# Cross-attention on one core: scores as fp32 matmuls on row halves, projections as 64-column tiles, both placed behind the scores of a step

## The reference, cut to what matters

```python
# x: (1, 1024, 128), ctx: (1, 6404, 128), 16 heads of 64, all fp32
Q, K, V = x @ W_Q, ctx @ W_K, ctx @ W_V        # split into 16 heads of 64 columns
scores = einsum('bhqd,bhkd->bhqk', Q, K) / 8
attn = softmax(scores)                          # over 6404 keys
context = einsum('bhqk,bhkd->bhqd', attn, V)
out = context @ W_O + x
return (out - mean) / sqrt(var + 1e-5)
```

## Time and profile before

| | |
|---|---|
| time, median of 3 runs | 1790.04 us (1789.16 to 1790.11) |
| span of the profiled execution | 1789.5 us |
| around the span | 0.5 us by the median; the page has no time of its own for the profiled execution |
| TensorE busy, share of the span | 99% |
| DVE, ACT busy | 71%, 52% |
| granted TensorE clock, mean | 0.998 (2.4 GHz level) |

### The profile page before, as it was taken

The page is one execution under the profiler, slowest core; times in us unless marked ns, Lnnn a source line. Parts: engine busy times, 40 slices in busy tenths (PEclk is TensorE's granted clock), DMA queues, the critical chain, the costliest instruction groups (busy, mean ns, idle before and its releaser), DMA issues.

```text
span 1789.5 us, 23718 instructions
## 1 busy us (share of the span) xinstructions
PE 1767.2 (99%) x7814; PEld 973.5 (54%) x7814; DVE 1266.8 (71%) x1376; ACT 931.8 (52%) x1079; POOL 21.3 (1%) x24
## 2 busy tenths in 40 slices
PE   9999999999999999999999999999999999999997
PEld 4555555555555555555555555555555555555555
DVE  5667667668667686667876677676786677776687
ACT  5555555555555555545555554555555555555552
POOL 0000000000000000000000000000000000000000
PEclk9999999999999999999999999999999999999999
DMA  2000000000000000000000000000000000000000
GB/s 80 12 18 18 13 21 18 12 18 12 22 18 18 12 22 15 17 18 12 22 18 12 18 18 17 18 18 12 18 22 12 18 18 12 16 18 12 18 1 13
DMA packets 25022, 31.41 MB, mean 18 GB/s; under 512 B 6384, under 2 KB 12528, under 8 KB 24944
## 3 DMA queue, kind: packets, MB, share of 16 engines
q1 hardware_dynamic: 24256, 29.78, 6.2%
q10 hardware_dynamic: 688, 0.66, 0.1%
HBM read 29.90 MB, written 0.52 MB: 17 GB/s over the span
## 4 chain that ended last, share of the span: by engine, by line
PE 98%; DVE 1%; issue 0%; DMA 0%; ACT 0%; POOLq 0%; POOL 0%; ACTq 0%
PE s_ps L442 44%; PE o_ps L453 41%; PE v_ps L430 5%; PE kq_ps L419 5%; PE kq_ps L425 1%; PE v_ps L577 0%; DMA xT_sb<-in_xT 0%; PE kq_ps L577 0%; DVE inv_sum L897 0%; PE o_ps L593 0%; DVE limits L841 0%; PE o_ps L425 0%; PE v_ps L593 0%; PE kq_ps L593 0%; PE s_ps L425 0%
## 5 line engine op out<-in xcount | busy, mean ns | idle before, releaser
L697 ACT ACTIVATE probs<-s_ps 128x1024 f32<-128x1024 f32 x816 | 793.0, 1024 | 777.8 <-PE s_ps L442 755.2
L828 DVE TENSOR_TENSOR sums<-sums,probs 128x1024 f32<-128x1024 f32 (+1 forms) x800 | 935.0, 1218 | 3.7 <-issue 0.5
L442 PE MATMUL s_ps<-q_parts,k_parts 128*128 128x512 f32 x3264 | 860.4, 405 | 7.5 <-DVE inv_sum L897 6.1
L453 PE MATMUL o_ps<-probs,v_ring 128*64 128x512 f32 x3264 | 746.3, 599 | 0.0
L442 PEld LDWEIGHTS s_ps<-q_parts,k_parts 128*128 128x128 f32 x3264 | 576.9, 188 | 285.8 <-issue 170.5
L453 PEld LDWEIGHTS o_ps<-probs,v_ring 128*64 128x64 f32 x3264 | 215.8, 136 | 419.0 <-issue 417.9
L815 DVE COPY v_ring<-v_ps 128x256 f32<-128x256 f32 (+1 forms) x209 | 87.4, 418 | 473.4 <-PE v_ps L430 473.4
L430 PEld LDWEIGHTS v_ps<-wv_sb,ctx_ring 128*128 128x128 f32 x816 | 123.4, 190 | 64.8 <-issue 56.1
L430 PE MATMUL v_ps<-wv_sb,ctx_ring 128*128 128x128 f32 x816 | 124.5, 274 | 0.0
L419 PE MATMUL kq_ps<-ctx_ring,wk_sb 128*128 128x512 f32 (+1 forms) x208 | 104.9, 586 | 0.0
L797 DVE TENSOR_TENSOR k_parts<-kq_ps,k_parts 64x512 fp32r<-64x512 f32 (+1 forms) x104 | 70.0, 673 | 9.7 <-ACT k_parts L682 6.5
(11 more groups left out here) (54 smaller groups left out, 112.5 us busy)
## 6 DMA issues: line engine op xcount, KB each, us to landing
ctx_ring<-in_ctxT SPq DMA_DIRECT2D x96, 256.0 KB, 2.6
ctx_ring<-in_ctxT SPq DMA_DIRECT2D x8, 130.0 KB, 2.4
wq_dup<-in_wq SPq DMA_DIRECT2D x14, 64.0 KB, 2.1
wk_sb<-in_wk SPq DMA_DIRECT2D x8, 64.0 KB, 2.3
wv_sb<-in_wv SPq DMA_DIRECT2D x8, 64.0 KB, 2.8
xT_sb<-in_xT ACTq DMA_DIRECT2D x1, 512.0 KB, 6.1
x_sb<-in_x SPq DMA_DIRECT2D x1, 512.0 KB, 5.4
wo_sb<-in_wo SPq DMA_DIRECT2D x1, 512.0 KB, 6.4
```

The source lines that it names most:

```text
L442: last = nc.tensor.matmul(s_ps[:, head, q], k_parts[:, head, cols:cols + P], q_parts[:, parity, head, part, q], start=(part == 0), stop=(p ...
L453: last = nc.tensor.matmul(o_ps[rows, q], v_ring[:, v_at[0], v_at[1], rows], p_view[:, p_slot, head, q], start=start, stop=stop)
L697: nc.scalar.activation(p_view[:, p_slot, head, :], s_ps[:, head, :], ACT.Exp, scale=SCALE).then_inc(probs_ready, 1)
L828: nc.vector.tensor_tensor(out=sums[0:rows, parity, head, :], in0=sums[0:rows, parity, head, :], in1=p_view[0:rows, p_slot, head, :], op=AL ...
```

## The change

Scores become plain fp32 matmuls on row halves: K of head 0 lies in rows 0 to 63 and K of head 1 in rows 64 to 127 of one tile `k_sb`, Q likewise in `q_sb`. `s_ps` is now ordered by half of the queries, then head, and `scores`, the exponentials and the sums go by half of the queries (both heads of it) where they went by head. The high and low parts and everything that made them are gone: one copy on ACT takes a projection (`take_k`, `take_q`). Each projection is two 64-column matmuls in place of one of 128 columns; Q of the next pair takes two such pairs in place of four whole matmuls, at steps c and c+4 of the straight part. In TensorE's order both score blocks come first, then the projection, then V:

On ACT the copy of a projection comes behind the exponentials of both chunks, on DVE the copy of V behind the sums of A. The diff, cut to its core:

```diff
-            uses.update({(c, "mid"): ("q", 0), (c, "end"): ("q", 1), (c + 4, "mid"): ("q", 2),
-                         (c + 8, "mid"): ("q", 3), (c + 10, "mid"): ("k", 0)})
+            uses.update({(c, "mid"): ("q", 0), (c + 4, "mid"): ("q", 1), (c + 10, "mid"): ("k", 0)})
...
-        k_parts = sb("k_parts", [P, 2, RING_COLS], F32R)
-        q_parts = sb("q_parts", [P, 2, 2, 2, NQ], F32R)
+        k_sb = sb("k_sb", [P, RING_COLS])
+        q_sb = sb("q_sb", [P, 2, NQ])
...
-        q0_ps = [o_ps[:, 0:QH], o_ps[:, QH:NQ], s_ps[:, 1, 0:QH], s_ps[:, 1, QH:NQ]]
+        q0_ps = [o_ps[:, 0:QH], o_ps[:, QH:NQ]]
...
-                for copy in range(2):
-                    sp.dma_start(wq_dup[:, parity, :, copy, :], src_q).then_inc(w_loaded[parity], 16)
+                sp.dma_start(wq_sb[:, parity, :], w_q[:, cols]).then_inc(w_loaded[parity], 16)
...
-                nc.tensor.matmul(kq_ps[:, 0:n], wk_sb[:, parity, :], ctx_ring[:, b_slot * BK:b_slot * BK + n],
-                                 start=True, stop=True).then_inc(kq_proj_done, 1)
+                for head in range(2):
+                    rows = slice(head * DH, (head + 1) * DH)
+                    last = nc.tensor.matmul(kq_ps[rows, 0:n], wk_sb[:, parity, rows],
+                                            ctx_ring[:, b_slot * BK:b_slot * BK + n], start=True, stop=True)
+                last.then_inc(kq_proj_done, 1)
...
             def project_v(pos, cols, parity):
-                return nc.tensor.matmul(v_ps[:, pos * P:(pos + 1) * P], ctx_ring[:, cols:cols + P],
-                                        wv_sb[:, parity, :], start=True, stop=True)
+                for half in range(2):
+                    keys = slice(half * DH, (half + 1) * DH)
+                    last = nc.tensor.matmul(v_ps[keys, pos * P:(pos + 1) * P],
+                                            ctx_ring[:, cols + half * DH:cols + (half + 1) * DH],
+                                            wv_sb[:, parity, :], start=True, stop=True)
+                return last
...
             def scores(cols, parity, exps_before):
-                for head in range(2):
+                for h in range(NQH):
                     if exps_before is not None:
-                        pe.wait_ge(probs_ready, exps_before + head + 1)
-                    for h in range(NQH):
-                        q = slice(h * QH, (h + 1) * QH)
-                        for part in range(2):
-                            last = nc.tensor.matmul(s_ps[:, head, q], k_parts[:, head, cols:cols + P],
-                                                    q_parts[:, parity, head, part, q],
-                                                    start=(part == 0), stop=(part == 1))
+                        pe.wait_ge(probs_ready, exps_before + h + 1)
+                    for head in range(2):
+                        rows = slice(head * DH, (head + 1) * DH)
+                        last = nc.tensor.matmul(s_ps[:, h, head * QH:(head + 1) * QH], k_sb[rows, cols:cols + P],
+                                                q_sb[rows, parity, h * QH:(h + 1) * QH], start=True, stop=True)
                     last.then_inc(scores_ready, 1)
...
                 def step(c, k, looped):
                     todo = chunks_of(c, k)
-                    chunk_scores(*todo[0], looped)
+                    for following in todo:
+                        chunk_scores(*following, looped)
                     projection(c, k, looped, "mid")
...
                     group.then_inc(v_proj_done, 1)
-                    if len(todo) > 1:
-                        chunk_scores(*todo[1], looped)
...
-                nc.scalar.activation(k_parts[0:DH, 0, cols], kq_ps[0:DH, 0:n], ACT.Copy)
-                nc.scalar.activation(k_parts[DH:P, 1, cols], kq_ps[DH:P, 0:n], ACT.Copy).then_inc(kq_high_ready, 1)
+                nc.scalar.activation(k_sb[:, slot * BK:slot * BK + n], kq_ps[:, 0:n], ACT.Copy).then_inc(kq_taken, 1)
...
-                        if n == 0:
-                            high_halves(c, k, looped, "mid")
-                    high_halves(c, k, looped, "end")
+                    take_projection(c, k, looped, "mid")
+                    take_projection(c, k, looped, "end")
...
-            def low_k(slot):
-            def low_q(src, n, parity):
```

More of the change, by code:

```diff
@@ new lines, in project_k @@
+                last.then_inc(kq_proj_done, 1)
+            def project_q(dst, n, parity):
+                for head in range(2):
+                    rows = slice(head * DH, (head + 1) * DH)
+                    last = nc.tensor.matmul(dst[rows, :], wq_sb[:, parity, rows], xT_sb[:, n * QH:(n + 1) * QH],
+                                            start=True, stop=True)
+                last.then_inc(kq_proj_done, 1)
+            def project_v(pos, cols, parity):
+                for half in range(2):
[4 more added lines that the diff above has]
+                return last
@@ L452, in pv @@
                         rows = slice(head * DH, (head + 1) * DH)
-                        last = nc.tensor.matmul(o_ps[rows, q], v_ring[:, v_at[0], v_at[1], rows], p_view[:, p_slot, head, q],
-                                                start=start, stop=stop)
+                        last = nc.tensor.matmul(o_ps[rows, q], v_ring[:, v_at[0], v_at[1], rows],
+                                                p_view[:, p_slot, h, head * QH:(head + 1) * QH], start=start, stop=stop)
                 last.then_inc(pv_done, 1)
@@ L467, in _ @@
             project_k(0, 0, None)
-            pe.wait_ge(wq0_loaded, 32)
+            pe.wait_ge(wq0_loaded, 16)
             pe.wait_ge(x_loaded, 16)
-            for n in range(4):
+            for n in range(NQH):
                 project_q(q0_ps[n], n, 0)
@@ L569, in pair_body @@
                     if h == 0:
-                        pe.wait_ge(kq_split, use(pair, LOOP_USES + len(straight_uses(last)) - 1))
+                        pe.wait_ge(kq_taken, use(pair, LOOP_USES + len(straight_uses(last)) - 1))
                     else:
@@ L584, in w_need @@
                 if first:
[L585 to L586 removed]
+                    return 48
+                return 24 * pair + (16 + 24 if parity else 48)
             run_pairs(pe, pair_body)
@@ L818, in add_sums @@
             def add_sums(g, p_slot, parity, new, rows):
-                for head in range(2):
-                    dve.wait_ge(probs_ready, 2 * g + head + 1)
+                for h in range(NQH):
+                    dve.wait_ge(probs_ready, NQH * g + h + 1)
                     if new:
-                        nc.vector.tensor_copy(sums[:, parity, head, :], p_view[:, p_slot, head, :]).then_inc(sums_done, 1)
+                        nc.vector.tensor_copy(sums[:, parity, h, :], p_view[:, p_slot, h, :]).then_inc(sums_done, 1)
                     else:
-                        dve.wait_ge(sums_done, 2 * g + head + (SUM_CREDIT - 1))
-                        nc.vector.tensor_tensor(out=sums[0:rows, parity, head, :], in0=sums[0:rows, parity, head, :],
-                                                in1=p_view[0:rows, p_slot, head, :], op=ALU.add).then_inc(sums_done, 1)
+                        dve.wait_ge(sums_done, NQH * g + h + (SUM_CREDIT - 1))
+                        nc.vector.tensor_tensor(out=sums[0:rows, parity, h, :], in0=sums[0:rows, parity, h, :],
+                                                in1=p_view[0:rows, p_slot, h, :], op=ALU.add).then_inc(sums_done, 1)
             def invert_sums(pair, n):
@@ L853, in pair_body @@
                 g0 = CHUNKS * pair
-                def low_halves(c, k, looped, place):
-                    found = use_in(pair, c, k, looped, place, last)
-                    if found is not None:
-                        count, what, b, s = found
-                        dve.wait_ge(kq_high_ready, count)
-                        if what == "q":
-                            low_q(kq_ps[:, :], b, 1 - parity)
-                        else:
-                            low_k(s)
                 def step(c, k, looped):
                     todo = chunks_of(c, k)
-                    if k == 0:
-                        take_v(groups(pair, 0), v_place(1), 1, g0)
-                    else:
-                        alone = last and not looped and k + 2 == CHUNKS
-                        take_v(groups(pair, 0) + (c + 1) // 2, v_place(k + 1), 1 if alone else 2, g0 + c)
                     for n, (chunk, m) in enumerate(todo):
@@ L881, in step @@
                         if n == 0:
-                            low_halves(c, k, looped, "mid")
-                    low_halves(c, k, looped, "end")
+                            if k == 0:
+                                take_v(groups(pair, 0), v_place(1), 1, g0)
+                            else:
+                                alone = last and not looped and k + 2 == CHUNKS
+                                take_v(groups(pair, 0) + (c + 1) // 2, v_place(k + 1), 1 if alone else 2, g0 + c)
```

77 lines of the change are left out of this document (26 added, 51 removed).

## The result

The changed kernel takes 1840.43 us (median of 3 runs, 1840.21 to 1841.07) against 1790.04: 1.028 times as long, 95% interval 1.0268 to 1.0295. The forecast was 1832, slower. The span of the profiled execution went from 1789.5 to 1838.4, with the same mean clock of 0.998.

The account below looks back on a forecast made before the run. TensorE's block sequence was taken as the bound, with V just covering an exponential. Steps losing 57.5 us, less 12.0 (Q), 2.9 (start) and 1 (opening steps), gave +41.6 on 1789.5: 1831, median 1832, range 1803 to 1915.

Parts of the forecast that it names:

- What bounded the kernel: Whole span: TensorE's block sequence sets the end; V's 0.37 us between the score blocks exactly covers the exponential.
- Score matmuls: Score blocks: a row-half pair takes 0.43 us, first pair 0.11 extra; a chunk's pairs cost 1.72 against 1.84.
- Rivals (2): Score blocks: row halves overlap only in part, a pair 0.55 us, +0.7 a step, 1977 us; chance 0.05.
- (3): Score blocks: row halves do not overlap, +2.9 us a step, about 2400 us; chance 0.05.
- A and B side by side: A step's two score blocks: second starts at 2.25 us after 0.42 idle for the exponential, next block at 4.20.
- V behind B, pv: After the score blocks: V in sequence until 4.68 us, then pv 3.53, so a plain step ends at 8.21.
- Rival (4): V projections: their short column halves do not overlap, +0.43 us a step, 1918 us; chance 0.05.
- Borders: TensorE block borders: changing the array's form costs about 0.09 us, also between row and column halves.
- Rival (1): Block borders: form changes between half arrays cost nothing, steps gain 0.16 and 0.13 us, about 1746; chance 0.08.
- Q and the start: Q projections: 14 pairs replace 28 whole matmuls, 12.0 us saved; prologue before the first scores: 2.9 us saved.
- The sum: Whole span: 57.5 lost in steps, less 12.0, 2.9 and 1, gives +41.6 us on 1789.5.
- What was costed at nothing: DVE and ACT work, V copy, ctx reloads, DMAs and clock: zero cost, DVE not becoming the bound.

Follow-up runs that it names:

- Experiments 1: Changed kernel with the second score block put back behind the V projections on TensorE, new matmul forms kept: 1791.67 us, 1.0007 of the kernel before.
- experiments 2: Kernel before with both score blocks first and ACT and DVE in the changed order, old matmul forms kept: 1885.71 us, ratio 1.0531.
- 6: Changed kernel with only a step's K or Q projection put between the two score blocks, V staying behind: 1813.95 us, 1.0136 of the kernel before.
- experiment 4: Changed kernel with exponentials over only the first 512 of 1024 columns, TensorE's work unchanged: 1749.76 us, 0.9772 of the kernel before.
- Experiment 5: Changed kernel, all work kept, with the first score block's second half written to the idle PSUM banks of kq_ps and v_ps: 1722.33 us, ratio 0.9622.
- experiment 3: Changed kernel with all K, Q and V projections on the whole array again: 1883.32 us, 1.0518 of the kernel before.

## Why the prediction was right, point by point

**What bounded the kernel.** Right: TensorE's sequence, and in it the exponential that V covered to within 0.01 us. Experiments 1, 2 and 6 move the cover and the time follows; 4 shortens the exponential and 5 makes room for B, and the wait goes.

**Score matmuls.** A pair of records in 0.43, as taken; the second pair of a block 0.54 behind the first (815.51 - 814.97), the 0.11 at its upper bound. Rivals (2) and (3), partial or no overlap of row halves, are refuted by the rows above.

**A and B side by side.** B at 2.26 for 2.25. The end is 4.23 for 4.20. The difference lies mostly in B's second half. Its weights wait until 818.14, and I charged 0.03 for a later start of the half. Single records of the changed kernel, B's third and fourth pair and V's first:

```profile
818.19 0.65 PE L445 MATMUL s_ps<-q_sb,k_sb 64*128 64x512 f32 x2
818.67 0.60 PE L445 MATMUL s_ps<-q_sb,k_sb 64*128 64x512 f32 x2
819.20 0.33 PE L432 MATMUL v_ps<-wv_sb,ctx_ring 128*64 128x128 f32 x2
```

The half starts in time, 0.96 behind B as A's second half does behind A (0.97), but its record is 0.65 long instead of 0.60 and the pair after it comes 0.49 behind instead of 0.43. So this term was mis-sized: weights that come late cost the next pair 0.06 here, not 0.03.

**V behind B, pv.** 0.49 and 3.53, as summed. Rival (4), slow V halves, is refuted, and experiment 3 shows the halves to be worth 43 us.

**Borders.** Rival (1), free changes of form between half arrays, was the one that would have made the kernel faster. The last pair of `pv` starts at 814.45 and A at 814.97, 0.52 apart for a usual 0.43; B's last pair starts at 818.67 and V at 819.20, 0.53:

```profile
814.45 0.60 PE L455 MATMUL o_ps<-probs,v_ring 128*64 128x512 f32 x2
814.97 0.70 PE L445 MATMUL s_ps<-q_sb,k_sb 64*128 64x512 f32 x2
```

So a border costs 0.09 to 0.10 between two half forms too, as between half and whole, and the rival is refuted. The Trainium skill, "TensorEngine Tiling (Array Packing)", section "Key Properties", says that a change of tiling mode drains the engine; the 0.09 to 0.10 between row and column halves agree with this.

**Q and the start.** The scores of the first chunk start at 9.07 instead of 13.12: 4.0 saved for 2.9. The Q projection began at 6.46 instead of 8.04, 1.6 that the sum did not have; from there to the scores 2.6 pass instead of 5.1, which is 2.5 of the 2.9. The load of x is issued at 1.19 instead of 1.77 and takes 4.8 to land instead of 6.1. Changed kernel:

```profile
6.46 1.92 PE L424 MATMUL o_ps<-xT_sb,wq_sb 128*64 128x512 f32 x8
...
9.07 1.99 PE L445 MATMUL s_ps<-q_sb,k_sb 64*128 64x512 f32 x8 [0.47 <-ACT q_sb L684]
```

**The sum.** Forecast +41.6 on the span, measured +48.9. Steps are 0.04 longer than summed, 200 times: +8; the start -1; one wait of `pv` for the V copy, 0.8 us once, +1. That makes 49.6. The 84 and 116 steps are counts of the kernel before; in the changed one 109 have a projection, as its Q takes two steps of a pair and not three, and since the sum takes the Q matmuls out apart, this moves it little. What was costed at nothing stayed so but for that one wait: DVE and ACT have less work than before, no transfer is among TensorE's waits but one of 0.4 us at the start, and the clock is 1.00 in the step, where TensorE stands idle before B:

```profile
814.97:823.22 8.25, 7.98 (x42) 2.79 (x41) 5.05 (x5) 3.88 (x4) 0.00 (x0) 1.00 0.12 32
```

Experiment 5 gives back 0.59 us a step (3.64 for 4.23). Of this 0.49 is what experiment 4 gives back too (3.74 for 4.23): the wait of 0.43 and the 0.06 of B's second half. The other 0.10 is the first load of B, which in experiment 4 still waits for the exponential and in experiment 5 does not. The 0.06 is read from the rows alone; no run takes it away by itself.

## What to carry to other kernels

Work that stands between a producer's two bursts may be what hides the consumer's latency; before it is moved to save border or switching costs, lay the burst against the consumer's chain (end of the half, start of the exponential, its end, the next weight load) and see which comes later. A wait for a buffer of PSUM may be worth more when it is removed by using banks that are idle at that time than by reordering: here that was worth 118 us against 49 for undoing the move. A change of many parts can hold a gain and a larger loss, and what a part is worth can depend on another part; the square of two by two shows both.

## What the runs showed of the hardware that was not expected

The forecast took the pace of the row halves from the column halves without a row for it, and it held: with fp32 and 128-column weights a pair of records takes 0.43 us, though each pair needs two loads of 0.19, for the loads of the two halves run side by side. A short whole-array matmul followed by column halves costs some 0.10 at the border and not the 0.20 that experiments 2 and 3 expected. And a weight load that comes just in time is not free: in experiment 4 TensorE's matmuls had no recorded wait before B and 0.10 a step remained.
